# Merge product of the second layer moved behind the transposes of v on TensorE, in a fused window-attention and Laplacian kernel

## The reference, cut to what matters

```python
# layer 0, on windows of 8 x 8 pixels, 6 heads of 32 channels
qk, v = QK_w @ gn(x) + QK_b, V_w @ gn(x) + V_b           # 1x1 convolutions
o    = irfft2(rfft2(q * SCALE) * rfft2(k))               # per window, head and channel
attn = softmax(o @ v.T + position_bias)
x    = x + proj_w @ (attn @ v) + proj_b
# layer 1
edges = laplacian_3x3(gn(x))                             # per channel, zero padding
x    = x + merge_w @ (gn(x) + edges) + merge_b
```

## Time and profile before

| | |
|---|---|
| median of 3 runs | 6344.52 us |
| the profiled execution | 6342.08 us, span 6340.3 us |
| granted TensorE clock, mean | 0.993 |
| TensorE matmul busy | 6143.9 us (97%) |
| VectorE busy | 5402.9 us (85%) |
| ScalarE busy | 3755.0 us (59%) |
| GpSimd busy | 2148.4 us (34%) |

### The profile page before, as it was taken

The page is one execution under the profiler, slowest core; times in us unless marked ns, Lnnn a source line. Parts: engine busy times, 40 slices in busy tenths (PEclk is TensorE's granted clock), DMA queues, the critical chain, the costliest instruction groups (busy, mean ns, idle before and its releaser), DMA issues.

```text
span 6340.3 us, 224291 instructions
## 1 busy us (share of the span) xinstructions
PE 6143.9 (97%) x95748; PEld 5255.1 (83%) x95748; DVE 5402.9 (85%) x11877; ACT 3755.0 (59%) x9088; POOL 2148.4 (34%) x2310
## 2 busy tenths in 40 slices
PE   8999999999999999999999999999999999999987
PEld 6888788888888888888888888888888888888876
DVE  5777788888888888888888888888889888888876
ACT  3666666665666656665566655666556665566641
POOL 1333333333333333333333333333333333333320
PEclk9999999999999999999999999999999999999989
DMA  4121233333332233333233223333333322222325
GB/s 144 59 69 42 59 97 93 87 89 85 87 106 82 74 85 112 89 89 85 86 87 108 74 79 92 109 87 88 86 87 90 105 67 69 81 71 67 88 70 158
DMA packets 379003, 551.56 MB, mean 87 GB/s; under 512 B 23398, under 2 KB 283561, under 8 KB 365738
## 3 DMA queue, kind: packets, MB, share of 16 engines
q1 hardware_dynamic: 378028, 537.21, 30.0%
HBM read 335.80 MB, written 201.33 MB: 85 GB/s over the span
## 4 chain that ended last, share of the span: by engine, by line
PE 83%; DVE 15%; issue 1%; ACT 1%; SPq 0%; DMA 0%; POOL 0%; DVEq 0%; ACTq 0%
PE b_q L482 18%; PE b_t L534 11%; PE b_s L554 8%; PE b_o L523 6%; PE b_s L445 6%; PE b_s L513 5%; PE b_t L488 4%; DVE dg L688 3%; PE b_s L503 3%; PE b_s L501 3%; PE b_s L500 3%; PE b_s L502 3%; PE b_o L422 3%; PE b_o L424 2%; PE b_o L431 2%; PE b_o L433 2%
## 5 line engine op out<-in xcount | busy, mean ns | idle before, releaser
L975 POOL TENSOR_TENSOR probs<-probs,srec 128x384 f32<-128x384 f32 x1024 | 849.0, 829 | 3192.7 <-DVE srec L882 3192.7
L981 POOL TENSOR_TENSOR probs<-probs,smax 128x384 f32<-128x384 f32 x1024 | 930.4, 909 | 725.3 <-DVE smax L747 725.3
L742 DVE TENSOR_TENSOR probs<-b_s,posb 128x384 f32<-128x384 f32 x1024 | 558.0, 545 | 398.6 <-PE b_s L554 397.6
L890 ACT ACTIVATE probsT<-b_s 128x384 f32<-128x384 f32 x1024 | 502.1, 490 | 502.6 <-PE b_s L445 502.6
L482 PE MATMUL b_q<-wnh,xh 128*128 128x288 f32 x2048 | 762.3, 372 | 1.3 <-DVE xhl L853 1.3
L890 ACT ACTIVATE qh<-b_t 94x384 f32<-94x384 f32 x1024 | 498.4, 487 | 438.9 <-PE b_t L534 438.9
L831 DVE TENSOR_TENSOR qkl<-b_q,qkh 128x384 fp32r<-128x384 f32 x1024 | 566.2, 553 | 185.3 <-ACT qkh L890 166.4
L839 DVE SCALAR_TENSOR_TENSOR late<-b_s,pb,xs 128x128 f32<-128x128 f32 (+1 forms) x2048 | 612.4, 340 | 112.3 <-PE b_s L503 92.0
L890 ACT ACTIVATE vs<-b_q 128x192 f32<-128x192 f32 x1024 | 335.0, 327 | 627.5 <-PE b_q L482 627.5
L554 PEld LDWEIGHTS b_s<-vT,osb 32*64 32x64 f32 x24576 | 449.7, 132 | 293.1 <-ACT osb L890 254.4
L890 ACT ACTIVATE qkh<-b_q 128x384 fp32r<-128x384 f32 x1024 | 502.1, 490 | 301.2 <-PE b_q L482 281.6
(11 more groups left out here) (160 smaller groups left out, 15200.2 us busy)
## 6 DMA issues: line engine op xcount, KB each, us to landing
ld<-in_x SPq DMA_DIRECT2D x96, 1024.0 KB, 5.1
late<-x_dram SPq DMA_DIRECT2D x112, 640.0 KB, 6.4
xs<-in_x SPq DMA_DIRECT2D x128, 512.0 KB, 5.7
x_dram<-late SPq DMA_DIRECT2D x128, 512.0 KB, 2.8
out<-late SPq DMA_DIRECT2D x128, 512.0 KB, 4.7
late<-x_dram SPq DMA_DIRECT2D x240, 192.0 KB, 6.6
xs<-in_x SPq DMA_DIRECT2D x128, 256.0 KB, 6.4
x_dram<-late SPq DMA_DIRECT2D x128, 256.0 KB, 3.5
```

The costliest lines, as they stand in the source:

```text
L742: V.tensor_tensor(scored(i).rearrange("p (t w) m -> p t w m", w=2), scores.rearrange("p (t w m) -> p t w m", w=2, m=N), posb[:, :, :].unsq ...
L890: return A.activation(o, i, ACT.Copy)
L975: P.tensor_tensor(probs[:, i % 3, :, :], probs[:, i % 3, :, :], srec[:, i % 2, :].unsqueeze(2).broadcast_to([128, 6, N]), ALU.mult).then_i ...
L981: P.tensor_tensor(probs[:, i % 3, :, :], probs[:, i % 3, :, :], smax[:, i % 2, :].unsqueeze(2).broadcast_to([128, 6, N]), ALU.subtract).th ...
```

## The change

The ten QKV products and the two transposes of v, which stood behind the merge piece, now stand in front of it. Nothing else is touched: the same instructions run with the same waits, and no other engine's list changes. The first section of the diff (the block `if pair(0):`) is the same text as the one removed further down.

```diff
@@ -446,6 +446,27 @@
                     last.then_inc(pT_mm, 1)
+                if pair(0):
+                    i, n = pair(0)
+                    h, par = i // 4, i // NP % 2
+                    at = slice(i % 4 * 128, i % 4 * 128 + 128)
+                    products = [(xh, wnh, 0), (xh, wnl, 0), (xhb, wnh, 1), (xl, wnh, 0), (xhl, wnl, 1)]
+                    if i % 4 == 0:
+                        pe.wait_ge(xh_done, 3 * (h + 1))
+                        pe.wait_ge(xl_done, h + 1)
+                        pe.wait_ge(xhl_done, h + 1)
+                    for lo, up, done in ((QKV // 2, QKV, v_mm), (0, QKV // 2, qkv_mm)):
+                        o = b_q[:, first + lo:first + up]
+                        for k, (xx, ww, t) in enumerate(products):
+                            last = mm(o, xx[:, h % 2, at], ww[:, par, t, lo:up], start=(k == 0), stop=(k == 4))
+                        last.then_inc(done, 1)
+                    pe.wait_ge(v_out, n)
+                    if pair(1):
+                        pe.wait_ge(prod_done, n - 1)
+                    for t in range(2):
+                        last = nc.tensor.transpose(vt_out[:, t, :],
+                                                   vs[:, i % 5, t * N:t * N + 128], ident[:, :])
+                    last.then_inc(vT_mm, 1)
                 task = m_task(it)
                 if task:
                     kind, at, p = task
@@ -467,27 +488,6 @@
                         group_spread(at)
                     else:
                         bias(at, p)
-                if pair(0):
...
-                    last.then_inc(vT_mm, 1)
                 if pair(5):
                     i, n = pair(5)
```

## The result

The changed kernel takes 6963.43 us (median of 4 runs, 6962.41 to 6965.06) against 6343.45 us for the kernel before on the same chip: the ratio is 1.0978, with a 95% interval of 1.0959 to 1.0997. It is 620 us slower. The forecast was 6982 us.

A forecast was written before the change was run, and what follows sets the result against it. The prediction took TensorE to set most passes and VectorE some. 6342.1 us profiled, plus 628 us for passes of 110 blocks and 12 us for small tasks, made 6982 us; range 6800 to 7120.

The forecast's parts named there:

- The bound before: TensorE sets most passes, VectorE some; VectorE has 0.72 us a pass free, and a longer wait makes it the bound.
- When the piece is ready: Readout starts at a + 3.06 in slots 0 to 3, a + 3.49 in 4 and 5; a is VectorE's bias add (L742).
- The added wait on VectorE: At the readout L727, 1.59 us in slots 0 to 3, 2.02 in 4 and 5; 1144 us in 110 blocks.
- The diagonal: VectorE's slot-2 diagonal, slow beside GpSimd's `xl`, now runs after it: 1.08 us a block back, 119 us in all.
- From `qkl` to the next add: End of each pass: 1.94 us in most slots, 3.10 in slot 3 and 2.40 in slot 5.
- Blocks without the read: The 40 of 110 blocks without VectorE's statistics read lose 4.51 us each, against 6.40 in the other 70.
- Small tasks: The 52 small tasks' readouts are put back by 0 to 1.6 us each: 12 us taken, bounds 0 to 83.
- The sum: Blocks' passes add 628 us and small tasks 12 to the profiled 6342.1 us: 6982 us.
- TensorE's idle time before L534: TensorE idles for `qkl` before the forward transform in nearly each such pass, some 600 us in all.
- piece becomes cover: Rival: the piece covers TensorE's 64 us of waiting for `qkl`, giving 6278 us, or 6342 without gain; chance 0.04.
- The floor of 6730: VectorE's added 1144 us less all its free time, 637, and the quick diagonals, 119: 388 us, so 6730 us.
- The room that the range left for a lower clock: TensorE's clock, granted at 1.00 before, might change with TensorE busy 88%; room was left at the range's top.

The follow-up runs named there:

- run 1: The changed kernel with VectorE's readout of the piece and of the small tasks moved behind `qkl`: 6581.06 us, ratio 1.0376.
- run 6: The kernel before, with GpSimd's `xl` issued in slots 3 and 7 instead of 2 and 6: 6287.30 us, ratio 0.9910.
- run 9: The changed kernel with GpSimd's `xl` issued in slots 3 and 7 as well: 6960.88 us, ratio 1.0980.
- run 8: The change for the merge pieces alone, the 52 small tasks staying in front of QKV: 6946.97 us, ratio 1.0952.
- run 3: The changed kernel with the piece between QKV and v's transposes, and VectorE's readout behind `qkl`: 6323.27 us, ratio 0.9970.
- run 2: The changed kernel with the piece between QKV and v's transposes, VectorE left as in the changed kernel: 6541.06 us, ratio 1.0313.
- run 4: The kernel before, with only VectorE's readout of the piece moved behind `qkl`: 6509.49 us, ratio 1.0265.

## Why the prediction was right, point by point

- **The bound before**: right. VectorE had 0.72 us a pass to spare, and a longer wait put it on the chain: 35% against 15%. TensorE still has 61%, so the changed kernel's passes run through both engines in turn.
- **When the piece is ready**: *a* + 3.06 and 3.49 were forecast; 3.02 to 3.07 and 3.51 were measured. A slot that already had the new order in the trace of before gave this number to some hundredths.
- **The added wait on VectorE**: 1144 us forecast, 1072 us of idle time measured. The Trainium skill's rule ("PSUM — Partial Sum Buffer", Engine vs sequencer instructions) holds here: L696 and L588, which need nothing of the piece, stood behind L727 for 1.47 us and did not pass it; in run 1, in front of it, they have no idle time before them. So run 1 shows that it is the place in the queue that costs.
- **The diagonal**: forecast to come back to 0.82 us, measured 0.823; run 6 shows the cause and run 9 that the change uses it up. In the changed kernel this credit hides part of the loss.
- **From `qkl` to the next add**: 1.94 us in the slots that TensorE ends (3464.65 to 3466.58 is 1.93). The two tails of VectorE were over-sized: 2.96 instead of 3.10 in slot 3, 2.12 instead of 2.40 in slot 5. I had read both from passes in which the residual (L839) still waited for the projection: it started 0.59 and 0.66 us behind `qkl`, against 0.46 and 0.45 in the changed kernel, where the projection is over by then. These are most of the 0.62 us a block by which 42.04 exceeds the measured 41.42.
- **Blocks without the read**: 180 us forecast for 40 of them; run 8, without the small tasks, has 195 there and 408 in the 70 others (448). A plain block without the read lost 4.0 us (4.51 forecast), and one of strip 13 7.8; my sum had treated all alike.
- **Small tasks**: 12 forecast, 16 measured (run 8).
- **The sum**: 640 forecast, 620 measured. The blocks with the read were put too high by 40 us, those without it and the small tasks too low by 15 and 4. That the total came within 20 us is in part luck.
- **TensorE's idle time before L534**: about 600 us forecast, 299 measured. The size was off. TensorE also idled before the transposes, which wait for `prod`: 207 us before L467, 146 of them for `prod` in slots 0 and 4. So the time is spread over two places.
- **Rivals**: "piece becomes cover" failed as argued, since L727 stands in front of `qkl`. In run 1 and in run 3 TensorE's wait for `qkl` does nearly go (under 4 us in the whole run), but run 1 pays more for the uncovered transposes, and run 3, with the transposes behind the piece, gains 20 us, not 64. The floor of 6730 was not approached, because in the changed order TensorE can't run ahead (run 2 shows that it could otherwise).

## What to carry to other kernels

Moving a producer later on one engine moves every wait on its result, and the price is read on the consumer's list: what stands behind the reader, and who waits for that. Before such a move, look for a pass in the trace that already has the new order; it gives the new ready time directly. And an instruction moved behind one that waits for its own consumer's engine loses the chance to run ahead when that engine is late.

## What the runs showed of the hardware

A VectorE instruction with two inputs in SBUF and a GpSimd instruction slow one another, in either direction. In the kernel before the diagonal came second to `xl` and took 1.90 us instead of 0.82. `xl` was itself second there, to L704 (3176.94, also with two inputs in SBUF, 0.09 us before it), and took 1.72 us; L704 kept its 0.68. The groups of `xl` in the stretch, before and in the changed kernel (there no such instruction runs beside it, and each takes about 1.27 us):

```profile
L987 POOL TENSOR_TENSOR xl<-xs,xh 128x512 fp32r<-128x512 f32 x219 | 330.6, 1510 | 0.0
L987 POOL TENSOR_TENSOR xl<-xs,xh 128x512 fp32r<-128x512 f32 x219 | 277.8, 1269 | 0.0
```

In run 4, where the stencil runs earlier, GpSimd's subtraction is the one that suffers. It took 1.67 us beside L696, and 0.83 us in slot 7, where only the product and a statistics read of VectorE ran beside it:

```profile
3272.12 1.67 POOL L989 TENSOR_TENSOR probs<-probs,smax 128x384 f32<-128x384 f32 x1 [1.11 <-DVE smax L778]
3272.41 0.68 DVE L696 TENSOR_TENSOR late<-dg 128x512 f32<-128x512 f32 x1
```

Its mean over that whole kernel is 1650 ns, against 909 before. ScalarE's exponential behind it waited 127 us for it in the whole run, against 36 before; whether that costs time no run tells. The Trainium skill ("SBUF — State Buffer", Who interferes with whom) calls the shared ports of the two engines an exclusive lock and says that issue order decides who blocks. For the diagonal and for `xl` the trace agrees. For this subtraction it does not quite: it started 0.29 us before L696 and was still the one that took twice its time, while L696 had its usual 0.68 us. The measured rows decide; I have no run that separates the reasons.

TensorE's clock was granted at 0.99 in the long stretch of the changed kernel, where TensorE idled 299 us before L534 and 207 us before L467. The room that the range left for a lower clock was not needed.
